# Cross attention in rounds of two steps, with scores and transposes on four shared PSUM banks

## The reference

```
q = x @ Wq + bq                    # 128 x 1024, 16 heads of 64 (x layer-normalised in the kernel)
k = ctx @ Wk + bk                  # 2048 x 1024
v = ctx @ Wv + bv                  # 2048 x 1024
logits  = einsum('bshd,bShd->bhsS', q, k) / 8
weights = softmax(logits, axis=-1)
attn    = einsum('bhsS,bShd->bshd', weights, v)
out     = attn @ Wo + bo
```

## Time and profile before

| | us |
|---|---|
| median of 3 runs (1481.35 to 1483.1) | 1481.84 |
| the profiled execution | 1481.26 |
| its span in the trace | 1479.5 |
| TensorE busy in the span | 1425.7 |
| VectorE busy | 753.0 |
| ScalarE busy | 487.3 |

### The profile page before, as it was taken

How to read it: one execution, slowest core, us unless ns; L and a number is a source line. 1 busy time by engine, 2 the same in 40 slices (tenths; PEclk the granted TensorE clock), 3 DMA queues, 4 the chain that set the end, 5 groups by cost and what they waited for, 6 DMA issues and landing times.

```text
span 1479.5 us, 22668 instructions
## 1 busy us (share of the span) xinstructions
PE 1425.7 (96%) x8596; PEld 1116.0 (75%) x8596; DVE 753.0 (51%) x1776; ACT 487.3 (33%) x1101; POOL 199.4 (13%) x164
## 2 busy tenths in 40 slices
PE   5999999999999999999999999999999888789999
PEld 4667778777877877787778777777787666678877
DVE  5335543463345335633543364345434646877769
ACT  3115531372144115611541273135213624222110
POOL 2321100130020003200100031011000333300030
PEclk9999999999999999999999999999999998799999
DMA  6511100150021003200200141011001320113200
GB/s 214 164 50 29 33 22 1 54 150 12 0 62 28 12 1 116 89 12 3 77 22 1 46 133 36 1 54 36 12 1 40 115 87 29 58 53 119 95 19 29
DMA packets 45817, 78.33 MB, mean 53 GB/s; under 512 B 6688, under 2 KB 14912, under 8 KB 44688
## 3 DMA queue, kind: packets, MB, share of 16 engines
q1 hardware_dynamic: 44192, 72.38, 15.8%
q0 software_dynamic: 1520, 4.51, 0.9%
HBM read 71.63 MB, written 5.24 MB: 52 GB/s over the span
## 4 chain that ended last, share of the span: by engine, by line
PE 91%; DVE 4%; issue 1%; ACT 1%; DMA 1%; SPq 1%; POOL 0%; ACTq 0%; DVEq 0%
PE b_ps L1123 24%; PE b_ps L1101 24%; PE b_ps L483 9%; PE b_ps L1170 8%; PE b_ps L1139 7%; PE b_ps L1152 7%; PE b_ps L509 3%; PE b_ps L414 3%; PE b_ps L1111 2%; PE b_ps L1195 2%; DMA stage<-in_ctx 1%; PE b_ps L419 1%; ACT b_ctxT L1230 1%; PE b_ps L1163 0%; ACT t_prob L553 0%
## 5 line engine op out<-in xcount | busy, mean ns | idle before, releaser
L1123 PE MATMUL b_ps<-b_ctxT,wk 128*128 128x512 f32 x1536 | 390.0, 402 | 0.0
L1101 PE MATMUL b_ps<-wv,b_ctxT 128*128 128x512 f32 x1536 | 372.2, 401 | 11.2 <-DVE b_ctxT L1309 11.2
L1101 PEld LDWEIGHTS b_ps<-wv,b_ctxT 128*128 128x128 f32 x1536 | 288.9, 190 | 87.6 <-issue 22.4
L1123 PEld LDWEIGHTS b_ps<-b_ctxT,wk 128*128 128x128 f32 x1536 | 281.5, 188 | 86.8 <-issue 25.0
L1286 ACT COPY b_pT<-b_ps 128x512 f32<-128x512 f32 x128 | 75.0, 586 | 603.4 <-PE b_ps L1152 602.8
L1404 DVE COPY b_pT<-b_ps 128x512 f32<-128x512 f32 x128 | 88.3, 690 | 254.3 <-PE b_ps L1152 254.1
L1322 DVE COPY b_V<-b_ps 128x512 f32<-128x512 f32 x128 | 88.5, 692 | 247.3 <-PE b_ps L1101 247.3
L1280 ACT ACTIVATE b_prob<-b_prob,b_negm 128x512 f32<-128x512 f32 x256 | 182.9, 720 | 58.9 <-DVE b_negm L1425 58.9
L1419 DVE TENSOR_SCALAR_CACHE_REDUCE b_prob<-b_ps 128x512 f32<-128x512 f32 x256 | 166.5, 688 | 29.6 <-PE b_ps L1139 28.4
L1061 POOL TENSOR_TENSOR wk<-stage,wk 128x512 fp32r<-128x512 f32 x30 | 39.0, 1300 | 763.4 <-ACT wk L1238 763.4
L1152 PE MATMUL b_ps<-ident,b_prob 128*128 128x128 f32 x1024 | 133.5, 273 | 3.9 <-DVE b_pT L1404 3.6
(11 more groups left out here) (192 smaller groups left out, 1111.6 us busy)
## 6 DMA issues: line engine op xcount, KB each, us to landing
stage<-in_ctx SPq DMA_DIRECT2D x64, 256.0 KB, 2.9
b_wo<-in_Wo SPq DMA_DIRECT2D x8, 1024.0 KB, 5.7
stage<-in_Wk SPq DMA_DIRECT2D x30, 256.0 KB, 2.6
stage<-in_Wv SPq DMA_DIRECT2D x28, 256.0 KB, 3.2
b_q<-q_s SPq DMA_DIRECT2D x32, 128.0 KB, 3.1
stage<-in_self_w SPq DMA_DIRECT2D x16, 256.0 KB, 2.7
t_raw<-in_q_proj SPq DMA_DIRECT2D x16, 256.0 KB, 4.5
t_raw<-in_k_proj SPq DMA_DIRECT2D x16, 256.0 KB, 3.5
```

The source lines that it names most:

```text
L1101: mm = nc.tensor.matmul(ps[:, G.bank[item]], ctxT[:, a, k, n * P:(n + 1) * P], wv[:, w, k], start=m == 0, stop=m == len(terms) - 1)
L1123: mm = nc.tensor.matmul(ps[:, G.bank["k", t]], wk[:, i % 2, w, k], ctxT[:, a, k, s * BANK:(s + 1) * BANK], start=m == 0, stop=m == len(ter ...
```

## The change

Each engine's loop goes over rounds of two steps. TensorE's order in round t (even) becomes K(t), K(t+1), S(t-1), S(t), T(t-6), W(t-8), W(t-7), T(t-5), then the products of both steps. S and T no longer have banks of their own: S(t) and T(w) write banks 3 and 4 or 5 and 6 by parity (`half_bank`), so that S(t-1) and T(t-6) share the pair 3 and 4, and S(t) and T(t-5) the pair 5 and 6. New waits guard this: T waits for `s_out` of the score it overwrites, S for the copies of the transposes that it overwrites. ACT's and DVE's lists are reordered to match. The value chunks, which were put 4 each on four steps, are put 5, 6 and 5 on three rounds; the context chunks of the next batch and the attention weights of the next stage are split in other steps; the "ln" and "sx" pieces move to even steps; and the next stage's pieces have three banks instead of five in the last eight steps.

```
-TAIL_STEPS = {114: "lr0", 115: "lr1", 116: "lr2", 117: "lr3", 119: "lr4", 120: "gate", 121: "ln0 sx0", 122: "ln1", 123:
-              "sx1", 124: "ln2", 125: "sx2", 131: "sk0", 133: "sq0 tq0", 134: "sv0 sq1 const tk0", 135: "sk1"}
+TAIL_STEPS = {108: "lr0", 110: "lr1", 112: "lr2", 114: "lr3", 116: "lr4", 118: "gate ln0", 120: "sx0", 122: "ln1", 124:
+              "sx1", 126: "ln2", 128: "sx2", 131: "sk0", 133: "sq0 tq0", 134: "sv0 sq1 const tk0", 135: "sk1"}
...
-                self.products[half * h + 5 + n // SB].append(("v", h, n))
+                self.products[half * h + (4 if n < 5 else 6 if n < 11 else 8)].append(("v", h, n))
...
-        work += [(self.STEPS * b - 3 + n // 4 + n % 4 // 2, ("ctx", b, n)) for b in range(1, NB + 1) for n in range(NC)]
+        work += [(self.STEPS * b + (-3 if n < 4 else -2 if n < 7 else -1 if n < 12 else 0), ("ctx", b, n))
+                 for b in range(1, NB) for n in range(NC)]
+        work += [(self.TOTAL - 3 + n // 2, ("ctx", NB, n)) for n in range(NC)]
...
+        def half_bank(t, half):
+            return SCB + 2 * (t % 2) + half
...   # scores(t)
-                if t > 0:
-                    pe.wait_ge(s_out, 2 * t)
+                if t >= 2:
+                    pe.wait_ge(s_out, 2 * (t - 1))
+                if t >= 7:
+                    pe.wait_ge(te_done, t - 6)
+                    pe.wait_ge(to_done, t - 6)
...   # transpose_probs(w), each half
                     pe.wait_ge(exp_done, 2 * w + 2)
-                    if n >= 2:
-                        pe.wait_ge((te_done, to_done)[half], w)
+                    pe.wait_ge(s_out, min(2 * (w + G.LAG_TURN - 1) + half + 1, 2 * TOTAL))
+                    if w >= 2:
+                        pe.wait_ge((te_done, to_done)[half], w - 1)
...   # TensorE's loop
+            for t in range(0, LAST + 1, 2):
                 w = t - G.LAG_TURN
                 if t < TOTAL:
                     keys(t)
+                    keys(t + 1)
+                if 1 <= t <= TOTAL:
+                    scores(t - 1)
+                if t < TOTAL:
+                    scores(t)
                 if 0 <= w < TOTAL:
                     transpose_probs(w)
-                if 1 <= t <= TOTAL:
-                    scores(t - 1)
-                if w >= 2 and w % 2 == 0:
+                if w >= 2:
                     weigh(w - 2)
                     weigh(w - 1)
+                if 0 <= w < TOTAL:
+                    transpose_probs(w + 1)
...
```

More of the change, by code:

```diff
@@ L170, in __init__ @@
         for t in range(self.LAST + 1):
[L171 to L178, removed]
+            if t % 2 == 0:
+                for x in [("k", t), ("k", t + 1)] * (t < self.TOTAL) + self.products[t] + self.products[t + 1]:
+                    place(x)
+        banks.extend((3, 4, 5, 6, 7))
+        last.update({3: ("t", 0), 4: ("t", 1), 5: ("t", 0), 6: ("t", 1), 7: ("a",)})
         for x in self.rest:
@@ L1138, in scores @@
                         rows = slice(h * HD, (h + 1) * HD)
-                        mm = nc.tensor.matmul(ps[:, SCB + h], q[rows, i % 2, l], kst[rows, t % 2, a], start=m == 0, stop=m == 2)
+                        mm = nc.tensor.matmul(ps[:, half_bank(t + 1, h)], q[rows, i % 2, l], kst[rows, t % 2, a], start=m == 0, stop=m == 2)
                         if m == 2:
@@ L1271, in _, with turned_even @@
+            def turned_even(w):
+                act.wait_ge(t_psum, 2 * w + 1)
+                if 2 * w >= SLOTS:
+                    act.wait_ge(pv_done, 2 * w - SLOTS + 1)
+                nc.scalar.copy(pT[:, 2 * w % SLOTS], ps[:, half_bank(w, 0)].rearrange("p (m t) -> p m t", m=4)).then_inc(te_done, 1)
+            for t in range(0, LAST + 1, 2):
                 w, e = t - G.LAG_TURN, t - G.LAG_EXP
+                if t < TOTAL:
+                    keys_hi(t)
                 if 0 <= e < TOTAL:
-                    i, s = divmod(e, SB)
@@ L1274, in _ @@
[L1274 to L1281, removed]
@@ L1297, in _ @@
-                for item in chunks[2:] + [item for item in G.splits[t] if item[0] != "ctx"]:
+                    exponentials(e)
+                if t < TOTAL:
+                    keys_hi(t + 1)
+                if 0 <= w < TOTAL:
+                    turned_even(w)
+                for item in G.splits[t]:
+                    split_hi(item)
+                if 0 <= e + 1 < TOTAL:
+                    exponentials(e + 1)
+                if 0 <= w < TOTAL:
+                    turned_even(w + 1)
@@ L1298, in _ @@
+                for item in G.splits[t + 1]:
                     split_hi(item)
-                for item in G.products[t]:
+                for item in G.products[t] + G.products[t + 1]:
                     tail.scalar(act, X, item)
@@ new lines, in turned_odd @@
+            def turned_odd(w):
+                i, s = divmod(w, SB)
+                dve.wait_ge(t_psum, 2 * w + 2)
+                if 2 * w >= SLOTS:
+                    dve.wait_ge(pv_done, 2 * w - SLOTS + 2)
+                nc.vector.tensor_copy(pT[:, (2 * w + 1) % SLOTS], ps[:, half_bank(w, 1)].rearrange("p (m t) -> p m t", m=4)).then_inc(to_done, 1)
+                if s == SB - 1:
+                    dve.wait_ge(exp_done, 2 * SB * (i + 1))
+                    nc.vector.tensor_reduce(total[:], sums[:, i % 2], AX.X, ALU.add).then_inc(total_done, 1)
+                    dve.wait_ge(total_done, i + 1)
+                    if i >= 2:
+                        dve.wait_ge(pv_done, ROUNDS * (i - 1))
+                    nc.vector.reciprocal(rinv[:, i % 2], total[:]).then_inc(rinv_done, 1)
+                    dve.wait_ge(rinv_done, i + 1)
@@ new lines, in _ @@
+            for t in range(0, LAST + 1, 2):
+                w = t - G.LAG_TURN
+                chunks = [[item for item in G.splits[n] if item[0] == "ctx" and item[2] % 2 == 0] for n in (t, t + 1)]
+                if t < TOTAL:
+                    keys_lo(t)
+                if 1 <= t <= TOTAL:
+                    scores_out(t - 1)
+                if t < TOTAL:
+                    scores_out(t)
+                if 0 <= w < TOTAL:
+                    turned_odd(w)
+                if t < TOTAL:
+                    keys_lo(t + 1)
+                for item in chunks[0]:
+                    chunk_rest(item[1], item[2])
+                if 0 <= w < TOTAL:
+                    turned_odd(w + 1)
+                for item in chunks[1]:
+                    chunk_rest(item[1], item[2])
+                if w > 0 and w % SB == 0:
+                    attention_out(w // SB - 1)
+                for item in G.products[t] + G.products[t + 1]:
```

128 lines of the change are left out of this document (54 added, 74 removed).

## The result

After the change the kernel takes 1492.64 us (median of 6 runs, 1490.48 to 1497.53) against 1482.47 (1480.3 to 1483.55) on the same chip. The ratio is 1.0081, 95% interval 1.0065 to 1.0096: slower by 0.8%. The forecast was 1482.7 and its range ended at 1492, 0.6 us under the result. The time lies near that of the second rival, ACT's queue at the batch borders, 1491.

The account below looks back on a forecast made before the run. The prediction took TensorE's own sequence to bound cross attention. On the profiled execution it summed 1481.3 - 18.0 (shape changes) + 24.4 (new wait) + 2.3 (borders) - 6.0 (end) - 1.3 (ln0) = 1482.7 us; range 1473 to 1492, 8 in 10.

Parts of the forecast that it names:

- the second rival: Batch borders: chunk loads queued on ACT delay the next batch's first keys, +10.5 us instead of +2.3, 1491; chance 0.22.
- Changes of shape: TensorE's regular round: four tile-shape changes instead of five, 11.13 us against 11.41; with the opening, minus 18.0 us.
- The opening: First three rounds of cross attention: K S K S becomes K K S S, saving 0.40 us each.
- The new wait: 61 rounds: T(t-6) waits for VectorE's readout of S(t-1), 0.40 us each, plus 24.4 us, bounds 18 and 30.
- The first and the third rival: Transposes wait 0.33 us, borders cost as before: 1476, chance 0.22; no wait, readout over earlier: 1458, chance 0.06.
- the fourth: Rival: grouping saves nothing, a bank change between two scores costs what a shape change does: 1501, chance 0.03.
- One sign: For the wait: L1152 idle about 0.2 us, ended by VectorE's L1419, in nearly every round; 12 to 20 us listed.
- Batch borders: Three borders where ACT splits next-batch chunks: 1.9 us lost each against 1.1 before, plus 2.3 us, bounds 0 and 10.
- The end: End of cross attention: splits two a step win back most of 9.0 us lost; minus 6.0, bounds plus 1, minus 8.
- the 2 us that the forecast left open: Self attention and experts after cross attention: other banks there may give 2 us either way.
- ln0 two steps ahead of sx0: Near the end of cross attention: the earlier ln0 piece takes away a 1.33 us wait, minus 1.3 us.

Follow-up runs that it names:

- experiment 3: Changed kernel with both weighings ahead of both transposes in every round (K K S S W W T T): 1481.96 us, 1.0009 to the kernel before.
- experiment 8: Changed kernel with load, split and low part of batches 1 to 3's context chunks cut to one eighth of the width: 1481.2 us, 0.9999.
- experiment 2: Changed kernel with cross attention's weight pieces (wk, wv) split one step earlier: 1484.43 us, 1.0033 to the kernel before.
- experiment 1: Changed kernel with the context chunks of batches 1 to 3 put back on their old steps: 1500.27 us, 1.0129 to the kernel before.
- Experiment 12: Kernel before with the two end edits alone: TAIL_STEPS spread by the change, next stage's attention weights split two a step: 1480.34 us, 0.9997.
- Experiment 7: Changed kernel with weighing ahead of the first transposes in round 128 alone: 1489.07 us, 1.0049 to the kernel before.

## Why the prediction was wrong

- **Changes of shape: right.** The forecast round was 11.13 us without the wait. Measured it is 11.51 less the wait of 0.39 (next point), 11.12. With one change less and no wait the round was 10.97 (experiment 3). The opening was overrated: of three rounds that should save 0.40 each, two saved 0.41 and the first nothing, and round 6 takes 0.36 more.
- **The new wait: right.** From the first scores to the transposes it is 177.74 - 175.91 = 1.83, where 1.59 pass from scores to weighing when nothing waits (experiment 3), and the first transposes take 1.17 to weighing against 1.02 where their banks were free (experiment 8, after the border's wait). That is 0.24 + 0.15 = 0.39 a round, forecast 0.40. Counted from the scores the halves start at 1.83 and 2.41; forecast were 1.77 to 1.87 and 2.38 to 2.48. Both terms together were forecast at +6.4 us and came to +5.4. The first and the third rival, a shorter wait or none, fell with it, and so did the fourth: two scores in a row take 1.59, forecast 1.60. One sign was misnamed: the wait is written as "issue".
- **Batch borders: the step that failed.** It said +2.3 us for three borders, and they measured +10.0. Its chain was the right one for the first of the two rounds (ACT's list, POOL's chunk, the load, the high keys), but every link was priced from quiet rows. ACT reached the chunks at 11.83 us of the round (forecast 11.9) and could have split the last piece at 17.4; it did at 18.57, since POOL's chunk took 1.6 and not 1.31, and the load 3.9 and not 2.9. The 2.9 was the median of the chunks' loads; the page before has 3.2 for those of in_Wv. Three more loads are issued in the same 4 us; that they lengthen it was not tested. S(t) then starts at 20.6, not 19.4. The second round was "about 1.1 us again" and came to 1.7 over a regular one. At the second border half clock followed the wait, 2.9 us that no term held. The result lies at the step's upper bound of 10, the value stood in its lower quarter. The rival with these rounds as its place gave +10.5. That its time, 1491, fits is in part luck, as it had the wrong half of a mechanism: it had the next batch's first keys held up by late chunks. In the changed kernel those keys never wait; the high keys do, behind the last weight pieces (experiment 2), and then behind chunks. Held-up keys are what experiment 1 shows.
- **The end: the second step that failed.** Forecast -6.0, measured -1.8 to the kernel's end, and only -0.7 of it in the stretch that was priced (from K(126) to the last pair of projections, the 24 matmuls of L414 or L413: 44.07 us before, 43.38 after); the other -1.1 came in self attention, inside the 2 us that the forecast left open. It counted on two splits a step to bring back most of 9.0 us of idle time and half clock. Experiment 12 shows that the spread itself doesn't: the same stretch took 44.92 us, as the waits move to other instructions in the lists. The new order leaves a wait of 2.91 where 1.0 was forecast; the step didn't write out VectorE's list in front of the last readout. Experiment 7 gets 4.1 us of it back.
- **ln0 two steps ahead of sx0: right**, -1.3 forecast, -1.8 measured (-1.85 in experiment 12).

Borders 7.7 and end 4.2 too low, less 1.0 for the rounds, 0.8 for an earlier start and 0.5 for ln0: within rounding 9.5 us, the miss on the profiled execution (+10.9 against +1.4). The earlier start is scatter: the first keys start at 92.47 us here and at 94.12 and 92.64 in experiments 7 and 8, whose heads are the same. Why half clock follows one wait and not another stays open; the last section has what the traces show of it.

## What to carry to other kernels

When several steps become one round, write out each in-order engine's list for the fullest round, not for the regular one: the round with its wait got the price that blocks of the trace gave, 11.53 us for 11.51, and the loss came from items that now stand at the end of a twice as long list with something urgent behind them. Price such a list with the durations of its own crowded stretch (here 3.9 us for a load whose median is 3.2), and put whatever TensorE needs next ahead of what waits for a load. As made, with transposes straight behind scores, the grouping cost 10 us (1492.64 against 1482.47). With the weighing between scores and transposes, weight pieces a step earlier and ACT's and DVE's lists reordered, the kernel became 23 us faster than before (1458.13 against 1480.78). The 23 us are not the grouping's alone: ln0's 1.8 is in them, and the kernel before was not run with earlier weight pieces or reordered lists.

## What the runs showed that was not expected

- A wait of TensorE on another engine's semaphore can stand in the views as "issue": 12.3 us of it on L1157. The line that it waits for was found here by laying the other engine's rows beside the weight loads.
- Two waits alike, 2.39 and 2.44 us, in rounds alike: after the first the granted clock stayed at 2.4 GHz, after the second it was 1.2 GHz for some 6 us (mean clock 1.00 and 0.80 in the two rounds), in which scores took 1.65 for 0.96 and transposes 1.97 for 1.09. The second wait so cost 2.44 + 2.9 us, over twice its length. It isn't the length of the wait that decides: the third, 2.46 us, left full clock. In the trace of experiment 7, whose kernel is the same up to round 128, waits of 2.02 and 2.25 us at the first border left it too, and a shorter one of 1.84 us at the second was followed by half clock (the next scores took 1.65 us). So a forecast should price such a wait with and without half clock behind it.
- A regular round that is 0.54 us shorter should give some 32 us in 60 rounds. The kernel became 11 us faster (1.0081 to 1.0009); the other 21 were lost where the faster round met the same queue, in part to half clock: over the three rounds at the first border the mean clock was 0.89 and TensorE was busy 38.40 us, in the changed kernel 1.00 and 34.57 us (experiment 3).
